# A cross-attention and binarised FFN layer: from one batch a body to pairs of batches, gelu in place in double PSUM banks, one exponential a batch

## What is computed

```python
x = x + xattn(layernorm(x), ctx, ctx, mask, ...)   # q = layernorm(x) Wq wq_h + bq_h; k, v from ctx
                                                   # softmax over 64 keys, out = tile(attn v, 16) Wo
h = gelu(layernorm(x) @ (alpha1 * sign(w1)).T + b1)    # 256 -> 1024, exact gelu
x = x + h @ (alpha2 * sign(w2)).T + b2                 # 1024 -> 256
```

## Time and profile before

| what | us |
|---|---|
| median of 3 runs | 413.41 (412.19 to 414.05) |
| profiled execution | 413.81 |
| its span in the trace | 412.0 |
| busy: PE, DVE, ACT, POOL | 340.5, 331.0, 259.2, 310.3 |
| mean granted TensorE clock | 0.935 of full speed |

### The profile page before, as it was taken

The page is one execution under the profiler, slowest core; times in us unless marked ns, Lnnn a source line. Parts: engine busy times, 40 slices in busy tenths (PEclk is TensorE's granted clock), DMA queues, the critical chain, the costliest instruction groups (busy, mean ns, idle before and its releaser), DMA issues. The chain is left out here.

```text
span 412.0 us, 7933 instructions
## 1 busy us (share of the span) xinstructions
PE 340.5 (83%) x2381; PEld 229.7 (56%) x2381; DVE 331.0 (80%) x718; ACT 259.2 (63%) x486; POOL 310.3 (75%) x462
## 2 busy tenths in 40 slices
PE   5987553999979889797979888888897979799794
PEld 4534341575847465665656565656474747475662
DVE  2857462999998979797989898989898979888655
ACT  1049313687868677676776767676776758586570
POOL 1310306687898989989898988888899898986866
PEclk9965555899999999999999999999999999999998
DMA  8700100101020201111111111010202020101012
GB/s 258 272 0 1 52 1 0 52 1 52 2 100 4 86 19 56 46 51 51 51 51 51 51 51 51 28 74 0 102 0 102 0 102 0 51 0 51 2 53 102
DMA packets 9424, 21.39 MB, mean 52 GB/s; under 512 B 1720, under 2 KB 4928, under 8 KB 9408
## 3 DMA queue, kind: packets, MB, share of 16 engines
q1 hardware_dynamic: 8496, 21.14, 14.2%
q10 hardware_dynamic: 912, 0.05, 0.1%
HBM read 12.80 MB, written 8.39 MB: 51 GB/s over the span
## 5 line engine op out<-in xcount | busy, mean ns | idle before, releaser
L650 DVE SCALAR_TENSOR_TENSOR h_lo<-h_sb,h_scale,h_hi 128x512 f16<-128x512 f32 x128 | 114.0, 921 | 12.5 <-POOL h_hi L415 9.5
L1188 PE MATMUL psZ<-sgn2T,h_hi 128*128 128x256 f16 x512 | 116.2, 273 | 0.5 <-DVE sgn2T L854 0.2
L1188 PE MATMUL psZ<-sgn2T,h_lo 128*128 128x256 f16 x512 | 116.0, 273 | 0.0
L1174 PE MATMUL psY<-x_hi,sgn1T 128*128 128x512 f16 x256 | 98.1, 383 | 1.6 <-ACT sgn1T L622 1.6
L499 ACT ACTIVATE h_sb<-psY,b_col,alpha1x 128x512 f32<-128x512 f32 x128 | 94.5, 776 | 6.5 <-PE psY L1174 3.9
L1174 PE MATMUL psY<-x_lo,sgn1T 128*128 128x512 f16 x256 | 98.2, 383 | 0.0
L1124 PE MATMUL psW<-ident,xh 128*128 128x128 f32 x256 | 36.5, 288 | 47.5 <-POOL xh L400 47.5
L400 POOL TENSOR_SCALAR xh<-x,rstd,nmr 128x256 f32<-128x256 f32 x64 | 62.7, 989 | 3.4 <-issue 1.9
L1124 PEld LDWEIGHTS psW<-ident,xh 128*128 128x128 f32 x256 | 29.2, 146 | 59.4 <-POOL xh L400 56.9
L415 POOL TENSOR_SCALAR h_hi<-h_sb,h_scale 128x512 f16<-128x512 f32 x64 | 46.3, 726 | 20.4 <-PE psZ L1188 18.0
L1188 PEld LDWEIGHTS psZ<-sgn2T,h_hi 128*128 128x128 f16 x512 | 49.9, 97 | 13.7 <-DVE h_lo L650 4.6
(11 more groups left out here) (141 smaller groups left out, 538.3 us busy)
## 6 DMA issues: line engine op xcount, KB each, us to landing
x_in<-in_x SPq DMA_DIRECT2D x16, 512.0 KB, 3.2
out_x<-z_sb SPq DMA_DIRECT2D x15, 512.0 KB, 2.6
w_sb<-in_L_ffn_w SPq DMA_DIRECT2D x2, 1024.0 KB, 10.0
ctx_sb<-in_ctx SPq DMA_DIRECT2D x1, 1024.0 KB, 8.0
out_x<-z_sb SPq DMA_DIRECT2D x2, 256.0 KB, 2.2
wk_sb<-in_L_xattn_Wk SPq DMA_DIRECT2D x1, 256.0 KB, 3.0
wq_sb<-in_L_xattn_Wq SPq DMA_DIRECT2D x1, 256.0 KB, 3.3
wv_sb<-in_L_xattn_Wv SPq DMA_DIRECT2D x1, 256.0 KB, 8.1
```

The source lines that it names most:

```text
L650: nc.vector.scalar_tensor_tensor(out=h_lo[c % 4][:, :], in0=h_sb[c % 4][:, :], scalar=h_scale[:, :], in1=h_hi[c % 4][:, :], op0=ALU.mult, ...
L1174: last = nc.tensor.matmul(psY[c % 4][:, :], sgn1T[:, k, c * P:(c + 1) * P], part[slot][:, k, :], start=(n == 0), stop=(n == 2 * KD - 1))
L1188: last = nc.tensor.matmul(psZ[j // 2][:, (j % 2) * D:(j % 2 + 1) * D], part[c % 4][:, j * P:(j + 1) * P], sgn2T[:, c, :], start=(c == 0 an ...
```

## The change

The four single banks psY become two double ones, and a step of the hidden layer is now a quarter (two chunks). Gelu writes over its own input in PSUM; h_sb goes. ScalarE alone rounds, 1024 wide, from PSUM to h_hi; VectorE's h_lo is 1024 wide and reads the gelu in PSUM. h_hi and h_lo have four buffers each. A `second_product` takes a quarter. The bank is free again when h_lo has been computed.

All queues loop over pairs of batches (i, 0) and (i, 1), with the attention of the next two, (i, 2) and (i, 3), inside. The score maximum is subtracted by GpSimd (`shift`), so that one exponential of 256 does for a batch; its row sums are a reduce of VectorE (`sum_e`) and their scaling goes from VectorE to GpSimd (`scale_sums`). The turned e of two batches is copied at once. Buffers of the attention are doubled. x is loaded a second time for the residual (`load_res`) into the space of the context, so a load of x waits only for its normalisation.

In the setup, TensorE turns the float32 weights and ScalarE takes the signs from PSUM, where VectorE made signs first and TensorE turned those in float16. The two maxima over partitions are a transpose, a reduce and a matmul each, in place of GpSimd's reduces. The attention of the first two batches runs ahead of the loop. Order of GpSimd there: norm of x 0 and 1, shifts, scalings, norm of x1 0, norms of x 2 and 3, norm of x1 1, b2 sum 0.

The banks and the loop of all queues (the old loop is in the listing above):

```diff
-psY = [stack.enter_context(nc.psum_tensor(f"psY{n}", [P, 512], F32)) for n in range(4)]
+psY = [stack.enter_context(nc.psum_tensor(f"psY{n}", [P, 2, 512], F32)) for n in range(2)]
...
+def pipeline(eng, pair):
+    pair(0)
+    pair(1)
+    with eng.Fori(2, PAIRS - 2) as i:
+        pair(i)
+    pair(PAIRS - 2)
+    pair(PAIRS - 1)
+    pair(PAIRS)
```

SyncE, the queue of loads and stores:

```diff
     def load_x(i, par):
+        wait(sp, normed[0], val(i, par - 2, 1, 1))
         sp.dma_start(x_in[par % 2][:, :, :], x_v[i * 2 + par, :, :, :]) \
           .then_inc(x_loaded[par % 2], 16)
+    def load_res(i, par):
+        wait(sp, x1_ready, val(i, par - 2, 1, 1))
+        sp.dma_start(x_res[par % 2], x_v[i * 2 + par, :, :, :]) \
+          .then_inc(res_loaded[par % 2], 16)
+    def store(i, par):
...
+    def pair(i):
+        for par in (2, 3):
+            if has(i, par):
+                load_res(i, par)
+        for par in (4, 5):
+            if has(i, par):
+                load_x(i, par)
+        if has(i, 0):
+            if has(i, -1):
+                store(i, -1)
+            store(i, 0)
+        else:
             for n in range(2):
                 sp.wait_ge((out_ready, out_half_ready)[n], (B, 1)[n])
                 sp.dma_start(out_v[B - 1, :, 2 * n:2 * n + 2, :],
                              z_sb[(B - 1) % 2][:, 2 * n:2 * n + 2, :]) \
                   .then_inc(out_stored[(B - 1) % 2], 16)
```

GpSimd:

```diff
+    def shift(i, par):
+        m = par % 2
+        wait_apart(pool, sc_maxed, val(i, par, 1, 1))
+        nc.gpsimd.tensor_tensor(sc[m][:, :, :], sc[m][:, :, :],
+                                nmax[m][:, :].unsqueeze(2).to_broadcast([P, T, SK]),
+                                ALU.add).then_inc(sc_shifted, 1)
+    def scale_sums(i, par):
+        m = par % 2
+        wait_apart(pool, e_summed, val(i, par, 1, 1))
+        nc.gpsimd.tensor_scalar(esum_scaled[m][:, :], esum[m][:, :], mv_scale[:, 1:2], E_SCALE,
+                                ALU.mult, ALU.mult).then_inc(esum_used, 1)
...
+    def pair(i):
+        if has(i, 2):
+            shift(i, 2)
+        if has(i, 0):
+            if has(i, -1):
+                add_residual(i, -1)
+            if has(i, 2):
+                shift(i, 3)
+            add_b2(i, 1)
+            if has(i, 2):
+                scale_sums(i, 2)
+                scale_sums(i, 3)
+            if has(i, 4):
+                norm(i, 4, 0, x_in[0])
+            if has(i, 2):
+                norm(i, 2, 1, x1[0])
+            add_residual(i, 0)
+            if has(i, 2):
+                norm(i, 3, 1, x1[1])
+            if has(i, 4):
+                norm(i, 5, 0, x_in[1])
+            if has(i, 2):
+                add_b2(i, 2)
+        else:
+            add_residual(i, -1, tiles=range(2), scaled=1)
+    pipeline(pool, pair)
```

ScalarE (the setup's last steps stand between its helpers and its loop):

```diff
+    def exp(i, par):
...
+        nc.scalar.activation(e_sb[m][:, :, :], sc[m][:, :, :], ACT.Exp).then_inc(exped, 1)
...
+    def copy_eT(i):
+        wait(act, attended, val(i, -1, 2, 2))
+        wait(act, e_turned, val(i, 1, 1, 1))
+        nc.scalar.activation(eT[:, :, :, :].rearrange("p b j t -> p (b j t)"),
+                             psW[0][:, :].bitcast(F16), ACT.Copy).then_inc(eT_copied, 1)
+    def gelu(i, par, c):
+        wait(act, y_ready, val(i, par, C, c + 1))
+        y = psY[c // 2 % 2][:, c % 2, :]
+        nc.scalar.activation(y, y, ACT.Gelu, bias=b1_col[:, c:c + 1],
+                             scale=alpha1x[:, c:c + 1]).then_inc(gelu_done, 1)
+    def round_h(i, par, q):
+        wait(act, z_added, val(i, par - 1, Q, q + 1))
+        wait(act, gelu_done, val(i, par, C, 2 * q + 2))
+        nc.scalar.activation(h_hi[q][:, :, :], psY[q % 2][:, :, :], ACT.Copy,
+                             scale=h_scale[:, :]).then_inc(h_hi_done, 1)
+    def hidden(i, par, q):
+        gelu(i, par, 2 * q)
+        gelu(i, par, 2 * q + 1)
+        round_h(i, par, q)
...
+    copy_eT(0)
+    signs_1()
+    signs_2()
+    row_sums_2()
+    copy_x1T(0, 0)
...
+    def pair(i):
+        if not has(i, 0):
+            return
+        hidden(i, 0, 0)
+        if first:
             copy_V(1)
+        if late:
+            copy_xT(i, 2, W)
+        if first:
             copy_V(2)
             copy_V(3)
+        hidden(i, 0, 1)
+        if late:
+            copy_xT(i, 3, W)
+        hidden(i, 0, 2)
+        copy_x1T(i, 1)
+        if late:
+            exp(i, 2)
+            round_e(i, 2)
+            exp(i, 3)
+            round_e(i, 3)
+        if first or second:
+            copy_V(4 + 2 * i)
+            copy_V(5 + 2 * i)
+        gelu(i, 0, 6)
+        gelu(i, 0, 7)
+        if late:
+            copy_eT(i + 1)
+        round_h(i, 0, 3)
+        hidden(i, 1, 0)
+        hidden(i, 1, 1)
+        hidden(i, 1, 2)
+        if late:
+            copy_x1T(i, 2)
+        hidden(i, 1, 3)
+    pipeline(act, pair)
```

VectorE:

```diff
+    def sum_e(i, par):
...
+        nc.vector.tensor_reduce(esum[m][:, :], e_sb[m][:, :, :], AX.X, ALU.add) \
...
+    def lo(i, par, q):
+        wait(dve, h_hi_done, val(i, par, Q, q + 1))
+        nc.vector.scalar_tensor_tensor(out=h_lo[q][:, :, :], in0=psY[q % 2][:, :, :],
+                                       scalar=h_scale[:, :], in1=h_hi[q][:, :, :],
+                                       op0=ALU.mult, op1=ALU.subtract).then_inc(h_lo_done, 1)
...
+    def pair(i):
         if prev:
+            lo(i, -1, 3)
+        if not has(i, 0):
+            scale_z(i, -1)
             dve.wait_ge(z_scaled, 2 * B)
             dve.wait_ge(x1b_ready, B)
+            m = (B - 1) % 2
             nc.vector.tensor_tensor(z_sb[m][:, 2:4, :], z_sb[m][:, 2:4, :], x1b[m][:, 2:4, :],
                                     ALU.add).then_inc(out_half_ready, 1)
+            return
+        if first:
+            copy_V(1)
+        if late:
+            split_xT(i, 2, W)
+        if first:
             copy_V(2)
             copy_V(3)
+        if late:
+            scores(i, 2, W[0])
+        lo(i, 0, 0)
+        if late:
+            mask_and_max(i, 2)
+            split_xT(i, 3, W)
+        lo(i, 0, 1)
+        if prev:
+            scale_z(i, -1)
+        if late:
+            scores(i, 3, W[0])
+            mask_and_max(i, 3)
+        lo(i, 0, 2)
+        split_x1T(i, 1)
+        if first or second:
+            copy_V(4 + 2 * i)
+            copy_V(5 + 2 * i)
+        if late:
+            split_e(i, 2)
+            split_e(i, 3)
+        if has(i, 4):
+            x_statistics(i, 4)
+        lo(i, 0, 3)
+        if late:
+            sum_e(i, 2)
+            sum_e(i, 3)
+            residual(i, 2, W)
+        lo(i, 1, 0)
+        if late:
+            x1_statistics(i, 2)
+        lo(i, 1, 1)
+        if late:
+            residual(i, 3, W)
+        scale_z(i, 0)
+        if late:
+            x1_statistics(i, 3)
+        lo(i, 1, 2)
+        if late:
+            split_x1T(i, 2)
+        if has(i, 4):
+            x_statistics(i, 5)
+    pipeline(dve, pair)
```

TensorE:

```diff
     def first_product(i, par, c):
+        q = c // 2
         if c == 0:
             wait(pe, lo_copied, val(i, par, KD, KD))
+        if c % 2 == 0:
+            wait(pe, h_lo_done, val(i, par, Q, q - 1))
         n = 0
         for k in range(KD):
             for part in (x_hi, x_lo):
+                last = nc.tensor.matmul(psY[q % 2][:, c % 2, :], sgn1T[:, k, c * P:(c + 1) * P],
+                                        part[par % 2][:, k, :], start=(n == 0), stop=(n == 2 * KD - 1))
                 n += 1
         last.then_inc(y_ready, 1)
...
+    def second_product(i, par, q):
+        if q == 0:
             wait(pe, z_scaled, val(i, par - 1, 2, 2))
+        wait(pe, h_lo_done, val(i, par, Q, q + 1))
+        for u in range(2):
+            for j in range(T):
+                for n, part in enumerate((h_hi, h_lo)):
+                    last = nc.tensor.matmul(psZ[j // 2][:, (j % 2) * D:(j % 2 + 1) * D],
+                                            part[q][:, u, j * P:(j + 1) * P],
...
+    def pair(i):
+        if prev:
+            second_product(i, -1, 1)
+        if not has(i, 0):
+            second_product(i, -1, 2)
+            second_product(i, -1, 3)
+            return
+        first_product(i, 0, 0)
+        first_product(i, 0, 1)
+        if first:
+            pe.wait_ge(x1_ready, 2)
+            values(1)
+            sum_alpha2()
+        if late:
+            wait(pe, lo_copied, val(i, 0, KD, KD))
+            wait(pe, normed[0], val(i, 2, 1, 1))
+            for k in reversed(range(KD)):
+                turn(0, 2, k, W[k])
+        if prev:
+            second_product(i, -1, 2)
+        if first:
+            pe.wait_ge(alpha2_ready, 1)
+            values(2)
+            pe.wait_ge(V_copied, 2)
+            values(3)
+        first_product(i, 0, 2)
+        if late:
+            score(i, 2, W[0])
+        first_product(i, 0, 3)
+        if late:
+            wait(pe, normed[0], val(i, 3, 1, 1))
+            turn(0, 3, 1, W[1])
+            wait(pe, sc_steps, val(i, 2, 3, 2))
+            turn(0, 3, 0, W[0])
+        if prev:
```

(115 more changed lines are left out.)

1000 lines of the change are left out of this document (406 added, 594 removed).

## The result

The changed kernel takes 425.45 us (median of 4, 422.09 to 426.68) against 413.73 for the kernel before: 1.0251 times as long, 95% interval 1.0215 to 1.0287. I forecast 393 and a gain. It is slower, and outside the range of 378 to 411.

What follows compares the result with a forecast made beforehand. GpSimd bounded the old body, TensorE next. TensorE's 35.7 us plus 4.6 of waits and gaps gave 40.3 a pair; 69.5 + 40 + 241.8 + 29 + 11.2 = 391.5, then 1.8 more: forecast 393 us, range 378 to 411.

Steps and rivals of the forecast that it cites:

- What is late next: One steady pair written out: TensorE's waits of 4.4 us, longest 1.8 for GpSimd's second norm; 40.3 us a pair.
- all at the granted clock of 1.00 that the loop has now: TensorE's matmuls in the loop, priced at full clock: 35.7 us a pair.
- a falling clock: TensorE's clock falling in the loop, listed among the signs that the forecast is wrong; no size or chance given.
- First pair 40, six pairs at 40.3: Loop part of the total: first pair 40 us, with V and alpha, then six pairs making 241.8 us.
- every price of a new form: New instruction forms: h_lo of 1024 at 1.28 us, rounding of 1024 at 1.11, gelu in PSUM at 0.78.
- the setup: Stretch before the loop: first hidden product at 69.5 us against 70.4, GpSimd's reduces gone; 65 or 73 possible.
- rival 5: Each Copy between exponentials and gelus brings a table load, 4 or more a pair; pairs of 43, about 413; chance 0.04.
- last pair and tail: End of the kernel: last pair without attention 29 us, then 11.2 from its last product to the end.
- GpSimd's sum: GpSimd's work a pair (norms, sums, shifts, scalings): 31 us taken; 37 or 41 with contended prices.
- rival 2: TensorE fully fed, its short waits gone: pairs of 36.5, total 366 us; chance 0.13.
- Rival 4: GpSimd still held up, four xh at 4.24 us delaying the x1 turn: pair 44.4, total 422, slower; chance 0.12.
- A period above 43 us: Sign that the forecast is wrong; above 43.1 a pair, xh at about 0.9 us, the held-up GpSimd case decides.

Runs made afterwards that it cites:

- z_first: Changed kernel with VectorE's z scaling of the pair's first batch ahead of the residual of batch i+3 instead of behind it; 410.61 us, 0.9885 of the kernel before.
- refill: Changed kernel with TensorE repeating first product 5 of the second batch three more times ahead of the z wait; 417.53 us, 1.004 of the kernel before.
- v_moved: Changed kernel with the products of values 4 to 7 all done in pair 0 in the two z banks; 423.15 us, 1.0168 of the kernel before.
- all3: Changed kernel with z scaling before the residual, row sums before the first batch's last h_lo, and values 4 to 7 in pair 0's z banks; 395.34 us, 0.9532.
- z_earlier: all3 with the z scaling one place further ahead on VectorE, before the second h_lo of the second batch; 394.96 us, 0.9548 of the kernel before.
- turn_late_z: z_earlier with first product 6 of the second batch ahead of the x1 turn, its gelu ahead of that turn's copy; 394.53 us, 0.9541.
- sums_early: Changed kernel with VectorE's two row sums ahead of the last h_lo of the pair's first batch instead of behind it; 419.95 us.

## Why the prediction was wrong

- **The step that failed** is the list of waits in "What is late next". It has TensorE at "the second of" GpSimd's norms at 33.7 us of the pair, with second_product(i, 1, 0) done before it. The last first product ahead of it does end at 32.4 (244.2 less the pair's start at 211.8), but that product needs scale_z(i, 0). The diff puts this behind residual(i, 3) in VectorE's queue, and it ends at 35.9. I wrote VectorE's order down for its sum and its h_lo and never asked who waits for the z scaling in the middle of a pair; in the kernel before no such wait appears among TensorE's. Its cost is 1.8 us in each of 7 pairs, 12.5 us: GpSimd's norm ends at 36.0 (35.5 forecast), but a double product of 1.75 now stands between the gate and the turn. z_first took 1.5 a pair back by this one edit, and with the row sums the pair is 39.64, under the 40.3 of the forecast. As a sum the pair of 42.08 is 36.6 of TensorE's own work (35.7 forecast), 3.4 of z wait (1.8 at the turn forecast) and 2.1 of other waits (2.6 forecast): the own work was 0.9 too low, hidden by the waits.
- **The same step, missed once more**: "all at the granted clock of 1.00 that the loop has now". The sum took waits as idle time alone. Five falls at 1.67 are 8.3 us; in refill, which fills the wait with work, there are none. I had named a falling clock among what would prove me wrong, but gave it no price and no chance.
- **First pair 40, six pairs at 40.3**: pair 1 was priced as a steady pair and carries four groups of V products. Beyond the two points above it lost 6.6 us, 3.2 by the block and its wait and 3.4 by the clock, which v_moved and all3 took back (50.3 to 43.5 and 39.5). Pair 0 lost 8.0 beyond them. Low clock behind the first product and behind the V block makes about 3 of it (eight first products in 3.37 and 3.10 us instead of 1.73), and waits for the second score (1.39) and for V's banks (1.86) some 3 more. The rest, some 2 us, stays open. Between these kernels pair 0 varies from 46.8 to 53.3 us, and most of that goes with its time at the low clock: 3.7 us of it in z_earlier (46.8), 6.5 in turn_late_z (48.5), 17.1 in z_first and sums_early (52.7 and 53.3).
- **Right**: every price of a new form; the setup (67.97 against 69.5, with no reduce in it); two table loads a pair, so rival 5 falls; last pair and tail within 0.2; GpSimd's sum, 28.3 us busy in a pair against 31. One reading was wrong without harm: the h_lo of 0.74 were not alone, they are the ones beside the xh of 4.24. Two slips change nothing: four sums of 2.8 are 11.2, not 11.4, and half way to rival 2 is 379.5, not 378.
- **Rival 4** had the sign and nearly the time (422), by a mechanism that isn't there: no xh took the 0.9 from which it decides (0.75 at most). The Trainium skill (SBUF — State Buffer, SBUF: two separate sides) would hold GpSimd up only beside VectorE ops with two SBUF inputs, of which few are left, or in a two-port mode; the trace agrees, with 0.554 as the mean of 64 xh. A period above 43 us was read in advance as GpSimd's; it was half queue order and half clock.

Against the kernel before the account is another one. The first products with which bodies 3, 5 and 15 start there, and pairs 1, 2 and 7 here:

```profile
112.89 0.39 PE L1174 MATMUL psY<-x_hi,sgn1T 128*128 128x512 f16 x1
155.55 0.38 PE L1174 MATMUL psY<-x_hi,sgn1T 128*128 128x512 f16 x1
370.35 0.38 PE L1174 MATMUL psY<-x_hi,sgn1T 128*128 128x512 f16 x1
```

```profile
119.39 0.38 PE L1202 MATMUL psY<-x_hi,sgn1T 128*128 128x512 f16 x1
169.71 0.38 PE L1202 MATMUL psY<-x_hi,sgn1T 128*128 128x512 f16 x1
384.93 0.38 PE L1202 MATMUL psY<-x_hi,sgn1T 128*128 128x512 f16 x1
```

| stretch | before | changed | difference |
|---|---|---|---|
| to the first hidden product | 70.4 | 68.0 | -2.4 |
| bodies 1 and 2, pair 0 | 42.5 | 51.4 | +8.9 |
| bodies 3 and 4, pair 1 | 42.7 | 50.3 | +7.7 |
| bodies 5 to 14, pairs 2 to 6 | 214.8 | 215.2 | +0.4 |
| the rest | 41.7 | 40.0 | -1.7 |

Where the clock holds, a pair of 42.1 is shorter than two bodies of 21.5, even with the z wait; three falls of 1.67 in the five later pairs use that up. What makes the kernel slower than before lies in its first two pairs. What makes it slower than forecast lies in all seven.

## What to carry to other kernels

When a loop is rewritten over larger units, list for every instruction that frees a bank who waits for it, and place it in its engine's queue by that, not next to its kin; a swap of two adjacent steps was worth 3.5% here. Price a wait of TensorE with the clock that may go behind it, and if the wait can't go, work put into it can pay. Read a pair's length from the trace of every variant, first and second iterations apart from the rest: the totals mixed three effects and the clock.
